# An adaptive-layer-norm block with log-sparse attention: other filler matmuls in the setup, the FFN weight's quantisation on ScalarE and GpSimd, and another order of ScalarE's and GpSimd's work in steps 0 to 2

## The chip, the cores and the metric

One core of a Trainium2 chip runs the kernel. The metric is the device time of one execution in microseconds (us), the median of three runs. A profiled execution gives the trace; its clock starts at the first instruction.

## The reference

Eight batches of 512 tokens by 256 channels (L = 512, D = 256), 16 heads of 16 channels, all in f32:

```python
mod = (silu(c) @ wmod).reshape(8, 6, 1, -1)      # sa, ca, ga, sb, cb, gb
ga, gb = sign * maximum(abs(.), 0.25)            # both gates
h = layernorm(x) * (1 + ca) + sa
q, k, v = h @ Wq.T + bq, h @ Wk.T + bk, h @ Wv.T + bv
scores = where(log_sparse_mask, q @ k.T, 0) / sqrt(16)   # j = i or j = i - 2**k
x = x + ga * (softmax(scores) @ v @ Wo.T + bo)
h = layernorm(x) * (1 + cb) + sb
x = x + gb * (dequant(fp6(h)) @ dequant(fp6(W)).T + bias)
```

`fp6` takes blocks of 32 values, scales each by its largest magnitude over 7.5 and rounds to the nearest of the 64 values of the format. A token attends with a score of its own to ten positions (itself and 1, 2, 4, ... 256 back); every other position counts with a score of zero.

## The kernel before, in words

**Setup.** The first batch is normalised, the weights are transposed by TensorE, and VectorE quantises the FFN weight (`setup_ffn_weight`: block maxima, scale, inverse, product, fp8 code, product back). Then VectorE makes the products of q and k of batch 0 (`first_qk_products`, L1710) and the rows of the modulation. TensorE fills waits with matmuls that nothing reads (`keep_busy`, three rows by 512 columns of bf16). GpSimd makes constants, the reciprocal root of batch 0 and later that of batch 1.

**Steps.** Then a loop of steps b = 0 to 5 runs on every engine, and an unrolled tail. Each engine's queue is written out by hand and runs in order; engines meet by semaphores alone. In step b:

- VectorE takes the maximum of the scores of batch b (L1802), subtracts it (L1806), waits for ScalarE's exponentials, makes the weights (L1819 to L1827), and then alternates the ten products of weights and v of batch b (`pv_product`, L1851) with the ten products of q and k of batch b + 1 (L1721).
- GpSimd adds the nine products of batch b to the first (`add`, L677), scales the projection's weight by the gate of batch b (`gate_projection`, L626), takes the reciprocal roots for batch b + 3 before attention and batch b - 1 after it (`rstd_before`, `rstd_both`), and from step 2 on modulates (L375, L380).
- ScalarE evacuates v, k, h and the attention from PSUM, takes sums and squares for both layer norms (L1188, L1197, L1217, L1238), normalises (`norm_before`, `norm_after`, L1174), takes the exponentials (`exps`), copies the scores of batch b + 1 (`copy_scores`, L1444, L1446) and puts q's bias into PSUM (`seed_q`).
- TensorE makes q and v of batch b + 1, transposes h of b + 2 and the attention of b - 1, projects, makes k of b + 2, sums the products over channels (`head_sums`, L937, L951) and transposes the scores (L963, L966).
- SyncE issues every transfer, in order: x of batch b + 3 (L414, after batch b + 2 is normalised), the spill of v and its seven shifted copies (L458, L466), each shifted copy after the product that frees its buffer, and between them rows such as the next gate row (L438), which waits for the gate product of batch b.

So in step b = 1 SyncE's order is: x of batch 4, spill of v, shifted copies 1 and 2, columns, copy 3, bias, residual x, copy 4, gate row of batch 2, copies 5, 6 and 7. Step 0 has the gate row of batch 1 in the same place, ahead of its copies 5 to 7.

Of the kernel before, what the change touches and what calls it, by code (L numbers as in the profile page):

```python
# [26 lines left out]
def adaln_block(nc, x, wq, bq, wk, bk, wv, bv, wo, bo, wf, bf, cond, wmod, out):  # L27
# [41 lines left out]
    with ExitStack() as ctx:  # L69
# [3 lines left out]
        def sem(name):  # L73
            return ctx.enter_context(nc.semaphore(name))
# [127 lines left out]
        s_xtile = sem("first_x_norm_tiles_by_scalar")  # L202
        s_xtiled = sem("first_x_norm_tiles_by_vector")
        s_split = sem("gated_biases_split")
        s_xin = sem("x_in_loaded")
# [84 lines left out]
        CONST_ALL = CONST_SUM + NO + 2  # L290
        SETUP_SILU, SETUP_COLS, SETUP_WF, SETUP_MOD, SETUP_ROWS = 3, 5, 11, 12, 16
        PE_COND, PE_MOD, PE_WK, PE_COLS, PE_WQ, PE_WV, PE_ROWS, PE_WO, PE_WF = range(1, 10)
# [276 lines left out]
        def _(pool):  # L569
# [25 lines left out]
            for n in range(1, NO):  # L595
# [5 lines left out]
                                    ALU.add).then_inc(s_const, 1)  # L601

            def split_gated_biases():

                pool.wait_ge(s_cset, SETUP_ROWS)
                nc.gpsimd.tensor_copy(split8[:, 0], gated8[:, :, :]).then_inc(s_split, 1)
                pool.wait_ge(s_split, 1)
                nc.gpsimd.tensor_tensor(rest8[:, :, :], gated8[:, :, :], split8[:, 0], ALU.subtract).then_inc(s_split, 1)
                pool.wait_ge(s_split, 2)
                nc.gpsimd.tensor_copy(split8[:, 1], rest8[:, :, :]).then_inc(s_split, 1)  # L610
                pool.wait_ge(s_split, 3)
                nc.gpsimd.tensor_tensor(rest8[:, :, :], rest8[:, :, :], split8[:, 1], ALU.subtract).then_inc(s_split, 1)
                pool.wait_ge(s_split, 4)
                nc.gpsimd.tensor_copy(split8[:, 2], rest8[:, :, :]).then_inc(s_split, 1)
# [79 lines left out]

            rstd_before(0)
            rstd_before(1)
            split_gated_biases()
            for b in range(LAST - 1):
                if has(b - 2):
                    modulate(pool, nc.gpsimd, b - 2)  # L700
                if has(b - 3):
                    gate_ffn(b - 3)
                if b == 0:
                    rstd_before(2)
                add(b, 1)
                add(b, 2)
                add(b, 3)
                add(b, 4)
                gate_projection(b)
                add(b, 5)  # L710
                add(b, 6)
                if has(b + 3) and has(b - 1):
                    rstd_both(b)
                elif has(b + 3):
                    rstd_before(b + 3)
                elif has(b - 1):
                    rstd_after(b - 1)
                add(b, 7)
                add(b, 8)
                add(b, 9)  # L720
            modulate(pool, nc.gpsimd, LAST - 3)
            gate_ffn(LAST - 4)
# [20 lines left out]
        @block.tensor  # L743
        def _(pe):
            pe.wait_ge(s_const, CONST_EARLY)
            for j in range(NC):
# [7 lines left out]

            keep_busy(ps67, 1, 3)
            pe.wait_ge(s_cond, 16)
            for k in range(NC):
                mm = nc.tensor.transpose(ps23[:, 0, B * k:B * k + B], cond_sb[:, P * k:P * k + P], ident[0:B, 0:B])
            mm.then_inc(s_pset, 1)
            keep_busy(ps67, 1, 4)  # L760

# [8 lines left out]
            def weight_transposes(i):  # L770

                pe.wait_ge(s_w_in[i], 16)
                if i == 2:
                    pe.wait_ge(s_cset, SETUP_COLS)
                if i == 3:
                    pe.wait_ge(s_d, 1)
                if i == 4:
                    pe.wait_ge(s_cset, SETUP_WF)
                    pe.wait_ge(s_x1, 1)
                for k in range(NC):  # L780
                    for c in range(NC):
                        mm = nc.tensor.transpose(turned_weight(i)[:, k, P * c:P * c + P], w_raw[:, i, c, P * k:P * k + P],
                                                 ident[:, :])
                mm.then_inc(s_pset, 1)
# [378 lines left out]
        def _(act):  # L1163
# [3 lines left out]
            def evacuate_weight(i):  # L1167
                act.wait_ge(s_pset, {2: PE_WV, 3: PE_WO, 4: PE_WF}[i])
                nc.scalar.activation(wT[:, i, :, :], turned_weight(i), ACT.Copy).then_inc(s_wTe, 1)

            def norm(src, dst, rstd, shift, done, tiles=slice(0, NT)):

# [280 lines left out]
            evacuate_weight(2)  # L1453
            evacuate_k(0, 0)
            sums_before(1)
            squares_before(1)
# [6 lines left out]
            seed_q(1)  # L1463
            centre_h(1)

            for b in range(LAST - 1):
                ahead, norm1 = has(b + 2), has(b + 3)
                exps(b)
                if has(b - 1):
                    mean_of_v(b - 1)  # L1470
# [5 lines left out]
                if has(b - 2) and has(b + 2):  # L1476
                    norm_after(b - 2)
                evacuate_v(b + 1, 1)
                if b == 0:
                    norm_before(2)  # L1480
# [12 lines left out]
                if has(b - 1):  # L1493
                    take_x1(b - 1)
                if ahead:
                    evacuate_k(b + 2, 1)
# [12 lines left out]
                if b == 1:  # L1509
                    evacuate_weight(4)  # L1510
                if has(b - 1):
                    squares_after(b - 1)
# [5 lines left out]
                if has(b + 2):  # L1518
                    seed_q(b + 2)
                if has(b + 3):  # L1520
                    norm_before(b + 3)
                elif has(b - 1):
                    norm_after(b - 1)
# [56 lines left out]
        def _(dve):  # L1580
# [87 lines left out]
            def setup_rows():  # L1668

                link, k = chain(s_cset, 0, 0)  # L1670
                k[0] = SETUP_WF
                dve.wait_ge(s_pset, PE_ROWS)
# [14 lines left out]

            def setup_ffn_weight():
                link, k = chain(s_cset, 0, 0)
                k[0] = SETUP_COLS  # L1690

                dve.wait_ge(s_w_in[4], 16)
                dve.wait_ge(s_const, 3)
                wf_b = w_raw[:, 4, :, :].rearrange("p c (g k) -> p (c g) k", k=BLOCK)
                wf_qb = wf_q[:, :].rearrange("p (g k) -> p g k", k=BLOCK)
                link(nc.vector.tensor_reduce(wf_amax[:, :], wf_b, AX_X, ALU.max, apply_absolute_value=True))
                link(nc.vector.tensor_scalar(wf_scale[:, :], wf_amax[:, :], TO_E4M3 / FP6_MAX, TO_E4M3 * MX_EPS,
                                             ALU.mult, ALU.max))
                link(nc.vector.reciprocal(wf_inv[:, :], wf_scale[:, :]))
                link(nc.vector.tensor_tensor(wf_b, wf_b, over(wf_inv[:, :], BLOCK), ALU.mult))  # L1700
                link(nc.vector.tensor_scalar(wf_q[:, :], w_raw[:, 4, :, :].rearrange("p c k -> p (c k)"), TIE_DOWN,
                                             None, ALU.add, saturate=False))
                link(nc.vector.tensor_tensor(wf_b, wf_qb, over(wf_scale[:, :], BLOCK), ALU.mult))
                assert k[0] == SETUP_WF

# [148 lines left out]

            setup_ffn_weight()
            first_qk_products(1)
# [106 lines left out]
```

## Time and profile before

| | |
|---|---|
| median of 3 runs | 286.82 us (286.75 to 286.82) |
| profiled execution, its own time | 286.72 us |
| its span | 285.0 us |
| busy: TensorE | 255.6 us (90%) |
| busy: VectorE | 258.8 us (91%) |
| busy: ScalarE | 212.5 us (75%) |
| busy: GpSimd | 210.5 us (74%) |
| maxima of scores (start of steps 0, 1, 2, 3 on VectorE) | 32.11, 59.49, 88.53, 117.86 us |

PE is TensorE's matmul queue, PEld its weight loads, DVE VectorE, ACT ScalarE, POOL GpSimd and SPq SyncE's queue of transfers. A busy share is a mean over the whole span; the timelines below are what shows who waits where.

### The profile page before, as it was taken

The page shows a single profiled execution, that of the slowest core. Times are in us where ns is not written, and L with a number is a line of the kernel's source. Part 1 is how long each engine was busy: PE and PEld are TensorE (multiplying, and loading weights), DVE is VectorE, ACT ScalarE, POOL GpSimd, SP SyncE. Part 2 cuts the span into 40 slices and gives each one's busy share as a digit, 9 for nine tenths or more (in the row PEclk, how much of TensorE's full clock was granted, in tenths as well). Part 3 has the DMA queues.
Part 4 walks back from the last instruction along what each step waited for, and adds up shares of the span by engine and source line. Part 5 has one row for each costly group of instructions (what it writes and reads, how often), then busy time and mean ns, then how long its engine had stood idle before and what let it go on. Part 6 is the DMA issues. An engine that isn't in the chain of part 4 may idle for free.

```text
span 285.0 us, 4442 instructions
## 1 busy us (share of the span) xinstructions
PE 255.6 (90%) x1368; PEld 158.8 (56%) x1368; DVE 258.8 (91%) x326; ACT 212.5 (75%) x577; POOL 210.5 (74%) x152
## 2 busy tenths in 40 slices
PE   6999997697978795989999999999999988997885
PEld 1653554175526561666556646664567646794663
DVE  3699799969995999999999999999999999999970
ACT  2386987975697779879898989887776937575752
POOL 7101439895879999999999999999999699845100
PEclk9999999999999999999999999999999999999999
DMA  7743977694784239724993389347943965730005
GB/s 225 193 181 81 340 248 232 230 338 133 240 273 148 73 125 350 251 72 131 295 336 127 129 263 286 135 113 222 333 147 94 279 198 178 230 103 11 0 26 199
DMA packets 54399, 53.91 MB, mean 189 GB/s; under 512 B 4100, under 2 KB 52824, under 8 KB 54376
## 3 DMA queue, kind: packets, MB, share of 16 engines
q1 hardware_dynamic: 54376, 53.63, 60.1%
q8 instruction: 11, 0.18, 0.3%
q14 instruction: 12, 0.10, 0.1%
HBM read 44.90 MB, written 8.72 MB: 188 GB/s over the span
## 4 chain that ended last, share of the span: by engine, by line
DVE 39%; POOL 19%; PE 18%; issue 11%; ACT 11%; DVEq 0%; POOLq 0%; ACTq 0%
POOL pv_buf L677 14%; DVE prod L1721 9%; DVE pv_buf L1851 9%; DVE prod L1851 4%; DVE prod L1710 4%; PE ps L988 3%; PE ps L1067 3%; PE ps L826 2%; ACT dump L1197 2%; PE ps L853 2%; ACT dump L1238 1%; DVE ps L1825 1%; PE ps L837 1%; DVE ps L1827 1%; POOL rstd L658 1%
## 5 line engine op out<-in xcount | busy, mean ns | idle before, releaser
L677 POOL TENSOR_TENSOR pv_buf<-pv_buf 128x1024 f32<-128x1024 f32 (+2 forms) x60 | 132.5, 2209 | 15.0 <-DVE pv_buf L1851 9.8
L1721 DVE TENSOR_TENSOR prod<-ps,kT 128x1024 f32<-128x1024 f32 (+4 forms) x70 | 75.1, 1110 | 0.0
L1851 DVE TENSOR_TENSOR pv_buf<-v_shift,ps 128x1024 f32<-128x1024 f32 x49 | 59.1, 1212 | 0.0
L937 PE MATMUL ps<-prod,sel_sum 128*32 128x512 f32 x256 | 30.8, 598 | 8.5 <-DVE prod L1721 7.8
L853 PE MATMUL ps<-wT,h_cen 128*128 128x256 f32 x128 | 29.9, 379 | 0.0
L826 PE MATMUL ps<-hT,wT 128*128 128x512 f32 x64 | 29.7, 596 | 0.0
L837 PE MATMUL ps<-hT,wT 128*128 128x512 f32 x64 | 29.3, 599 | 0.0
L988 PE MATMUL ps<-wo_g,w_raw 128*128 128x256 f32 x112 | 27.9, 392 | 0.0
L853 PEld LDWEIGHTS ps<-wT,h_cen 128*128 128x128 f32 x128 | 23.9, 190 | 6.4 <-issue 3.8
L988 PEld LDWEIGHTS ps<-wo_g,w_raw 128*128 128x128 f32 x112 | 20.1, 189 | 5.4 <-issue 3.2
L937 PEld LDWEIGHTS ps<-prod,sel_sum 128*32 128x32 f32 x256 | 6.7, 109 | 28.0 <-issue 13.8
L1067 PE MATMUL ps<-wf_g,w_raw 128*128 128x256 f32 x80 | 19.7, 391 | 0.0
L1851 DVE TENSOR_TENSOR pv_buf<-v_base,ps 128x1024 f32<-128x1024 f32 (+2 forms) x21 | 19.4, 950 | 0.2
L1291 ACT ACTIVATE kT<-ps,bias_cols 128x512 f32<-128x512 f32 x16 | 10.9, 686 | 11.6 <-PE ps L826 11.6
L649 POOL TENSOR_TENSOR rstd<-var,minus_half 128x4 f32<-128x4 f32 x4 | 4.1, 1016 | 20.1 <-ACT var L1201 19.3
L1174 ACT ACTIVATE x_norm<-x_in,shift,rstd 128x256 f32<-128x256 f32 x28 | 14.5, 594 | 5.6 <-POOL shift L651 3.2
L837 PEld LDWEIGHTS ps<-hT,wT 128*128 128x128 f32 x64 | 11.7, 190 | 12.4 <-issue 12.4
L826 PEld LDWEIGHTS ps<-hT,wT 128*128 128x128 f32 x64 | 11.6, 190 | 10.5 <-issue 9.0
L1067 PEld LDWEIGHTS ps<-wf_g,w_raw 128*128 128x128 f32 x80 | 14.5, 189 | 3.6 <-issue 2.0
L1174 ACT ACTIVATE x_norm<-x,shift,rstd 128x256 f32<-128x256 f32 x28 | 14.5, 592 | 1.4 <-POOL shift L668 1.4
L380 POOL TENSOR_TENSOR h<-x_norm,rows_mod 128x1024 f32<-128x1024 f32 x6 | 14.2, 2362 | 0.5
L375 POOL TENSOR_TENSOR x_norm<-x_norm,rows_mod 128x1024 f32<-128x1024 f32 x6 | 14.2, 2364 | 0.3 <-ACT x_norm L1174 0.2
(212 smaller groups left out, 550.3 us busy)
## 6 DMA issues: line engine op xcount, KB each, us to landing
v_shift<-v_rows SPq DMA_DIRECT2D x56, 512.0 KB, 5.7
x_in<-in_L_attn_x SPq DMA_DIRECT2D x8, 512.0 KB, 4.4
v_rows<-v_base SPq DMA_DIRECT2D x8, 512.0 KB, 4.1
x_res<-in_L_attn_x SPq DMA_DIRECT2D x8, 512.0 KB, 6.5
out_x<-outb SPq DMA_DIRECT2D x5, 512.0 KB, 5.8
rows_mod<-mod_rows SPq DMA_DIRECT2D x7, 256.0 KB, 3.4
x<-in_L_wmod SPq DMA_DIRECT2D x1, 1024.0 KB, 7.9
row_ga<-mod_rows SPq DMA_DIRECT2D x8, 128.0 KB, 4.9
```

The source lines that it names most:

```text
L375: ops.tensor_tensor(normed[:, t, :], normed[:, t, :], rows[:, 0:1, :].broadcast_to([P, n, D]), ALU.mult).then_inc(scaled, 1)
L380: ops.tensor_tensor(dst[:, t, :], normed[:, t, :], rows[:, 1:2, :].broadcast_to([P, n, D]), ALU.add).then_inc(done, 1)
L677: nc.gpsimd.tensor_tensor(dst, dst, ring(b, n)[:, t:NT, :], ALU.add).then_inc(s_add, 1)
L826: mm = nc.tensor.matmul(ps23[:, j, :], wT[:, 1, k, P * j:P * j + P], hT[:, k, :], start=(k == 1), stop=(k == 0))
L837: mm = nc.tensor.matmul(ps01[:, j, :], wT[:, 0, k, P * j:P * j + P], hT[:, k, :], start=False, stop=(k == NC - 1), skip_group_check=True)
L853: mm = nc.tensor.matmul(ps23[:, k2, col:col + D], h_cen[:, k, P * t:P * t + P], wT[:, 2, k, :], start=(t % 2 == 0 and k == 0), stop=(t % 2 ...
L937: mm = nc.tensor.matmul(ps23[32 * g:32 * g + 32, 1, :], sel_sum[:, which, c, :], prod[:, n, c, :], start=(c == 0 and which == 0), stop=(c ...
L988: mm = nc.tensor.matmul(ps[:, k2, col:col + D], attnT[:, k, P * t:P * t + P], wo_by[b][:, k, :], start=False, stop=(t % 2 == 1 and k == NC ...
L1067: mm = nc.tensor.matmul(ps[:, half_, col:col + D], xdT_by[b][:, k, P * t:P * t + P], wf_by[b][:, k, :], start=False, stop=(t % 2 == 1 and ...
L1174: ins = nc.scalar.activation(dst[:, t, :], src[:, t, :], ACT.Identity, scale=rstd[:, t:t + 1], bias=shift[:, t:t + 1])
L1721: nc.vector.tensor_tensor(prod[:, n, :, o:L], ps01[:, :, o:L], kT[:, b % 2, :, 0:L - o], ALU.mult).then_inc(s_prod, 1)
L1851: nc.vector.tensor_tensor(dst[:, t:NT, :].rearrange("p t (h e) -> p t h e", e=DH), v_n.rearrange("p t (h e) -> p t h e", e=DH), weights, A ...
```

## The change

TensorE's filler: three matmuls of the 128 by 128 identity with itself as soon as it is made, ahead of the matmuls that open q's banks; one where three thin fillers stood; three where four stood. VectorE keeps three operations of the FFN weight's quantisation; GpSimd takes the two products and ScalarE the fp8 code, joined by a new semaphore, and the weight's transposes in step 1 wait for it. On ScalarE the centring of h of batch 1 moves behind the exponentials of step 0. The normalising of batches 3 and 4 moves from the end of steps 0 and 1 into steps 1 and 2, behind the exponentials and the first evacuation of v. The squares of x1 of steps 1 and 2 move to right behind the taking of x1, ahead of k's evacuation, so the scores' copies follow other work. On GpSimd the gate product of steps 0 and 1 moves behind the last addition, and in step 0 the reciprocal root for batch 3 too, ahead of the gate.

```diff
@@ gpsimd
+            def scale_ffn_weight(src, factor, after):
+                pool.wait_ge(s_wfq, after)
+                nc.gpsimd.tensor_tensor(w_raw[:, 4, :, :].rearrange("p c (g k) -> p (c g) k", k=BLOCK),
+                                        src.rearrange("p (g k) -> p g k", k=BLOCK), over(factor[:, :], BLOCK),
+                                        ALU.mult).then_inc(s_wfq, 1)
...
             rstd_before(0)
+            scale_ffn_weight(w_raw[:, 4, :, :].rearrange("p c k -> p (c k)"), wf_inv, WF_SCALED - 1)
+            scale_ffn_weight(wf_q[:, :], wf_scale, WF_CODES)
             rstd_before(1)
...
                 add(b, 4)
-                gate_projection(b)
+                if b > 1:
+                    gate_projection(b)
                 add(b, 5)
                 add(b, 6)
                 if has(b + 3) and has(b - 1):
                     rstd_both(b)
-                elif has(b + 3):
-                    rstd_before(b + 3)
                 elif has(b - 1):
                     rstd_after(b - 1)
...
                 add(b, 9)
+                if b == 0:
+                    rstd_before(3)
+                if b < 2:
+                    gate_projection(b)
@@ tensor
+            def warm_up(ps, bank, n):
+                for i in range(n):
+                    nc.tensor.matmul(ps[:, bank, 0:P], ident[:, :], ident[:, :], start=True, stop=True)
+
+            pe.wait_ge(s_const, 2)
+            warm_up(ps67, 1, 3)
             pe.wait_ge(s_const, CONST_EARLY)
...
-            keep_busy(ps67, 1, 3)
+            warm_up(ps67, 1, 1)
             pe.wait_ge(s_cond, 16)
...
-            keep_busy(ps67, 1, 4)
+            warm_up(ps67, 1, 3)
...
                 if i == 4:
-                    pe.wait_ge(s_cset, SETUP_WF)
+                    pe.wait_ge(s_wfq, WF_DONE)
                     pe.wait_ge(s_x1, 1)
@@ scalar
+            def ffn_weight_codes():
+                act.wait_ge(s_wfq, WF_SCALED)
+                act.wait_ge(s_const, 3)
+                nc.scalar.activation(wf_q[:, :], w_raw[:, 4, :, :].rearrange("p c k -> p (c k)"), ACT.Identity,
+                                     bias=tie[:, 0:1], saturate=False).then_inc(s_wfq, 1)
...
             evacuate_k(0, 0)
+            ffn_weight_codes()
             sums_before(1)
...
-            centre_h(1)
...
                 exps(b)
+                if b == 0:
+                    centre_h(1)
...
                 evacuate_v(b + 1, 1)
+                if 0 < b < TAIL - 1:
+                    norm_before(b + 2)
...
                     take_x1(b - 1)
+                    if b < TAIL - 1:
+                        squares_after(b - 1)
...
-                if has(b - 1):
+                if has(b - 1) and b >= TAIL - 1:
                     squares_after(b - 1)
...
-                if has(b + 3):
+                if b >= TAIL - 2 and has(b + 3):
                     norm_before(b + 3)
-                elif has(b - 1):
+                elif b >= TAIL - 2 and has(b - 1):
                     norm_after(b - 1)
@@ vector
-                link(nc.vector.tensor_tensor(wf_b, wf_b, over(wf_inv[:, :], BLOCK), ALU.mult))
-                link(nc.vector.tensor_scalar(wf_q[:, :], w_raw[:, 4, :, :].rearrange("p c k -> p (c k)"), TIE_DOWN,
-                                             None, ALU.add, saturate=False))
-                link(nc.vector.tensor_tensor(wf_b, wf_qb, over(wf_scale[:, :], BLOCK), ALU.mult))
```

TAIL is 4. The three operations that stay on VectorE (maxima, scale, inverse) keep their place and form.

## Rows read from the trace of the kernel before

**Rows 1.** Chain of waits: start us, us, what.
```profile
14.63 0.70 DVE w_raw L1700
...
16.55 2.23 DVE prod L1710 x4
...
85.15 0.91 POOL pv_buf L677
...
123.60 1.06 PE ps L893 x8
```

**Rows 2.** Timeline, TensorE: start us, us, engine, line, op, out<-in, xcount.
```profile
3.19 1.48 PE L752 MATMUL ps<-ones 3*128 3x512 bf16 x3
...
9.37 1.97 PE L800 MATMUL ps<-ident,x_norm 128*128 128x128 f32 x8
...
11.12 1.06 PE L782 MATMUL ps<-ident,w_raw 128*128 128x128 f32 x4
...
12.17 1.95 PE L826 MATMUL ps<-hT,wT 128*128 128x512 f32 x4
...
13.96 1.88 PE L837 MATMUL ps<-hT,wT 128*128 128x512 f32 x4
...
29.50 1.09 PE L813 MATMUL ps<-ident,x_norm 128*128 128x128 f32 x8
```

**Rows 3.** Timeline, GpSimd, steps 0 to 2; in brackets the idle time before, and its releaser.
```profile
51.99 1.27 POOL L626 TENSOR_TENSOR wo_g<-wT,row_ga 128x512 f32<-128x512 f32 x1
...
69.25 7.39 POOL L677 TENSOR_TENSOR pv_buf<-pv_buf 128x1024 f32<-128x1024 f32 x3 [3.07 <-DVE pv_buf L1851]
...
85.15 2.36 POOL L677 TENSOR_TENSOR pv_buf<-pv_buf 128x1024 f32<-128x1024 f32 x1 [2.06 <-DVE pv_buf L1851]
```

**Rows 4.** One line's instructions: duration ns min/median/max, first and last start us.
```profile
L1421 ACT ACTIVATE q_last<-v_shift,tie x2: 722/722/722, 270.7 to 274.4; 128x512 fp8e4<-128x512 f32 x2
```

**Rows 5.** Timeline, VectorE and ScalarE, seams of step 0.
```profile
35.21 0.50 DVE L1819 TENSOR_TENSOR ps<-ps,em 128x320 f32<-128x320 f32 x1 [1.29 <-ACT ps L1433]
...
56.25 0.60 ACT L1444 ACTIVATE score_buf<-ps 128x512 f32<-128x512 f32 x1 [0.25 <-PE ps L937]
...
59.49 0.89 DVE L1802 TENSOR_REDUCE mx<-ps 128x64 f32<-128x704 f32 x1
```

**Rows 6.** Timeline, VectorE, waits for exponentials in steps 1 and 2.
```profile
63.49 0.50 DVE L1819 TENSOR_TENSOR ps<-ps,em 128x320 f32<-128x320 f32 x1 [2.19 <-ACT ps L1433]
...
92.41 0.50 DVE L1819 TENSOR_TENSOR ps<-ps,em 128x320 f32<-128x320 f32 x1 [2.06 <-ACT ps L1433]
```

**Rows 7.** Windows, GpSimd: stretch, its length, busy us (x instructions), clock, DMA.
```profile
88.00:117.00 29.00, 27.98 (x15) 1.00 0.59 192
```

**Rows 8.** Timeline, SyncE's queue, end of step 0 and step 1.
```profile
54.94 0.50 SPq L438 DMA_DIRECT2D row_ga<-mod_rows  x1
...
62.62 0.37 SPq L414 DMA_DIRECT2D x_in<-in_L_attn_x  x1
```

**Rows 9.** Timeline, ScalarE, step 1.
```profile
72.26 0.41 ACT L1188 ACTIVATE dump<-x_in 128x256 f32<-128x256 f32 x1
...
75.04 0.39 ACT L1217 ACTIVATE x<-ps 128x256 f32<-128x256 f32 x1 [0.36 <-PE ps L988]
...
76.75 0.69 ACT L1291 ACTIVATE kT<-ps,bias_cols 128x512 f32<-128x512 f32 x1 [0.87 <-PE ps L826]
...
78.47 0.69 ACT L1291 ACTIVATE kT<-ps,bias_cols 128x512 f32<-128x512 f32 x1 [1.03 <-PE ps L826]
...
82.97 0.58 ACT L1169 ACTIVATE wT<-ps 128x512 f32<-128x512 f32 x1
...
85.89 0.58 ACT L1444 ACTIVATE score_buf<-ps 128x512 f32<-128x512 f32 x1
```

**Rows 10.** Transfers into x_in, then into v_shift: us from issue to landing.
```profile
DMA to landing us min/median/max: 3.2/3.8/6.1
...
DMA to landing us min/median/max: 2.1/5.6/9.2
```

More of the change, by code:

```diff
@@ L203, in adaln_block @@
         s_xtiled = sem("first_x_norm_tiles_by_vector")
+        s_wfq = sem("ffn_weight_quantising_step")
         s_split = sem("gated_biases_split")
@@ L290, in adaln_block @@
         CONST_ALL = CONST_SUM + NO + 2
-        SETUP_SILU, SETUP_COLS, SETUP_WF, SETUP_MOD, SETUP_ROWS = 3, 5, 11, 12, 16
+        SETUP_SILU, SETUP_COLS, SETUP_MOD, SETUP_ROWS = 3, 5, 6, 10
+        WF_SCALED, WF_CODES, WF_DONE = 4, 5, 6
         PE_COND, PE_MOD, PE_WK, PE_COLS, PE_WQ, PE_WV, PE_ROWS, PE_WO, PE_WF = range(1, 10)
@@ L1670, in setup_rows @@
                 link, k = chain(s_cset, 0, 0)
-                k[0] = SETUP_WF
+                k[0] = SETUP_COLS
                 dve.wait_ge(s_pset, PE_ROWS)
@@ L1686, in setup_rows, with ffn_weight_scales @@
                 assert k[0] == SETUP_ROWS
-            def setup_ffn_weight():
-                link, k = chain(s_cset, 0, 0)
-                k[0] = SETUP_COLS
+            def ffn_weight_scales():
                 dve.wait_ge(s_w_in[4], 16)
-                dve.wait_ge(s_const, 3)
                 wf_b = w_raw[:, 4, :, :].rearrange("p c (g k) -> p (c g) k", k=BLOCK)
[L1695 to L1699, printed above, removed]
-                link(nc.vector.tensor_tensor(wf_b, wf_b, over(wf_inv[:, :], BLOCK), ALU.mult))
-                link(nc.vector.tensor_scalar(wf_q[:, :], w_raw[:, 4, :, :].rearrange("p c k -> p (c k)"), TIE_DOWN,
-                                             None, ALU.add, saturate=False))
-                link(nc.vector.tensor_tensor(wf_b, wf_qb, over(wf_scale[:, :], BLOCK), ALU.mult))
-                assert k[0] == SETUP_WF
+                nc.vector.tensor_reduce(wf_amax[:, :], wf_b, AX_X, ALU.max,
+                                        apply_absolute_value=True).then_inc(s_wfq, 1)
+                dve.wait_ge(s_wfq, 1)
+                nc.vector.tensor_scalar(wf_scale[:, :], wf_amax[:, :], TO_E4M3 / FP6_MAX, TO_E4M3 * MX_EPS,
+                                        ALU.mult, ALU.max).then_inc(s_wfq, 1)
+                dve.wait_ge(s_wfq, 2)
+                nc.vector.reciprocal(wf_inv[:, :], wf_scale[:, :]).then_inc(s_wfq, 1)
             def first_qk_products(c):
@@ L1853, in pv_product @@
                                         ALU.mult).then_inc(s_pv, 1)
-            setup_ffn_weight()
+            ffn_weight_scales()
             first_qk_products(1)
```

## The prediction

> **What bounds the kernel now.** I read four views in this order. The chain of waits comes first, since it says which engine sets the end in which stretch. In the setup it runs over VectorE: the FFN weight is scaled and quantised there, right ahead of the first products of q and k [rows 1]. Through steps 1 and 2 (up to about 123 us) it runs over GpSimd's additions, then it enters TensorE's transposes of the attention at 123.60 and stays on TensorE and ScalarE for the next two steps [rows 1]. So what the change gives early counts only as far as it moves the first q and k products and, later, GpSimd's last addition of step 2. Second, the timeline of TensorE in the setup shows its rate [rows 2]. Third, the timelines of GpSimd, VectorE and ScalarE show who waits at the seams of steps 0 to 2 [rows 3 to 6, 9]. Last, the SyncE queue and the landing times show what the moved gate holds back [rows 8, 10].
>
> All times below are on the clock of the profiled execution: span 285.0 us, its own time 286.72, so 1.7 us lie outside the span. The median of the runs is 286.82, 0.10 more. I subtract the gain from the median.
>
> **Setup: the FFN weight leaves VectorE.** Three of its six operations go (scale, code, scale back), 14.63 to 16.55: 1.92 us [rows 1]. They become a GpSimd product, a ScalarE activation and a second GpSimd product. GpSimd is idle then; a product of this shape takes 1.27 us there [rows 3], so the first runs from about 14.6 to 15.9. ScalarE's code operation, 0.72 us for this shape [rows 4], stands behind the second k evacuation and delays the statistics of batch 1; ScalarE waits for scores later in the setup, which hides it. The weight's transposes come only in step 1, so this route costs nothing as long as these idle stretches are there, and at most 0.7 us without them. The gain is not 1.92: VectorE would be free at 14.63, but the first product needs q. TensorE's four passes for it start at 13.96 and end at 15.84 [rows 2], after which 16.55 becomes 15.85. The floor of this term is 0.7 us.
>
> **Setup: deep instead of thin filler.** Seven fillers of 3 rows by 512 columns go, and seven of 128 by 128 come, two groups of them at other places. TensorE's rate is low until about 12.2: eight transposes take 1.97 us at 9.37, and eight of the same shape take 1.09 at 29.50 [rows 2]. The recorded granted clock says 1.00 for the whole span and does not show this, but spacings of 0.21 us against 0.11 are the two levels, 1.2 and 2.4 GHz. The thin fillers (three in 1.48 us) were running then [rows 2], and did not raise it; the rise came behind the full-height transposes at 9.37 and 11.12 [rows 2]. The fill is the one unknown of the setup. If the rise stays at 12.2, the term is 0.7. If it comes before 9.37, the eight transposes lose 0.9, the weight's four at 11.12 come at 10.4 and lose 0.5, q ends at 14.7 and the term is 1.8, with VectorE still in time (its three remaining weight operations end near 13.6). The new fillers are shorter in total, so they delay nothing; I bound a loss at 0.2 (one filler of 0.2 us in front of a real matmul). I take a rise inside the transposes, about 10.3: four of them and the weight's four run fast, q ends at about 15.3, term 1.2.
>
> The Trainium skill, page "TensorE: Matmul & The Clock Gate", section "Part 4: PE-mode transpose", says transposes don't engage the full clock, not counting as busy in the same way. The rows disagree: the work from 9.37 to 12.17 was transposes only, and the group at 12.17, four passes in 1.95 us, ran at the rate of every later one (0.43 us a pass) [rows 2]. By the page alone only the new real matmuls would count, which speaks for the early rise, 1.8.
>
> **Step 0: exponentials before centring.** VectorE waits 1.29 us for the exponentials, which stand behind the centring of h [rows 5]. They now start with the maximum, and VectorE goes on at about 34.0 instead of 35.21: some 1.25 earlier. But centring, k, and the statistics of batch 2 then end 0.4 later on ScalarE, and ScalarE is next: its first copy of scores stood at 56.25 after only 0.25 of waiting [rows 5]. With VectorE's products early and ScalarE 0.4 late, the second copy ends at about 57.5 instead of 57.7, and the maximum of step 1 starts at 59.3 rather than 59.49. Of 1.25 us 0.2 stay.
>
> **Step 1.** GpSimd no longer has the gate (1.27 us) and the root among its additions of step 0. It waited there for products anyway: the sixth addition can start with its product, 1.25 earlier than now, at 55.6, and ends at 58.0 by 2.36 us each [rows 3]; three more of 1024, 768 and 512 columns take 5.7. The last ends near 63.7 instead of 66.2 (69.25 less the wait of 3.07 [rows 3]), then the root ends at 65.0 and the gate at 66.25, inside that wait. ScalarE's exponentials no longer wait behind the normalising of batch 3: the 2.19 us at 63.49 [rows 6] go, and 0.2 from step 0 comes to it: VectorE runs 2.4 ahead in step 1. The normalising itself falls into ScalarE's wait for the attention's transposes.
>
> Now the queue. SyncE's load of the next gate row stood at 54.94 [rows 8]; it waits for the gate product, so it comes at 66.3, and with it three shifted copies of v (0.5 MB each) and the load of x for batch 4, which is 62.62 in the profile [rows 8] and becomes about 68.2. Landings of x take 3.2 to 6.1 us [rows 10]; behind four other transfers I take the upper end, 74.3. ScalarE would be ready for it at 71.5 (72.26 now [rows 9]), so a new wait of some 2.8 us arises. From there to the variance it has work of 85.89 - 72.26 = 13.6, less the three waits of 0.36, 0.87 and 1.03 and the weight's copy of 0.58, which now comes behind: 10.8 [rows 9]. It ends at 85.1. GpSimd's sixth addition, started at 85.15 now behind a wait of 2.06 for the product [rows 3], starts 2.4 earlier and ends at 85.1 too. So the new wait just fits, with nothing to spare, and the root starts at 85.1, 2.4 earlier than 87.5.
>
> **Step 2.** The wait of 2.06 for the exponentials goes as well [rows 6], but GpSimd is the engine that decides: from 85.15 it works without a pause into step 3, as its 27.98 busy microseconds of 29 show [rows 7] (the missing one is spread over the hand-overs), and the chain lies on it [rows 1]. The gate of step 1, which lay before a wait, now lies in the unbroken part: +1.27. 2.4 - 1.27 = 1.1 us earlier at the last addition, and so at the transposes of 123.60 [rows 1]. The gate row of step 2 and x for batch 5 are again late (x lands near 102, ScalarE waits 2), but its variance is due 1.8 before GpSimd asks. From step 3 on the order is the old one and the difference stays.
>
> **Sum.** 1.2 (setup) + 1.1 (steps 0 to 2) = 2.3; 286.82 - 2.3 = 284.5.
>
> **Rivals.**
> (a) The clock rises where it did: for it, the new fillers last 1.5 us in all against 3 for the thin ones, with gaps. 0.7 + 1.1: 285.0.
> (b) It rises before 9.37: 1.8 + 1.1: 283.9. For it, full-height work is what preceded the rise.
> (c) x of batch 4 arrives too late: slower. The place is ScalarE's sum at 72.26. From 74.3 on each microsecond goes on to GpSimd's root; the gain is used up at 76.6. Shifted copies of v took up to 9.2 us to land [rows 10]; with that, x lands at 77.4, 3.1 late: -2.3 + 3.1 = +0.8, 287.6, and a second late x in step 2 (9.2 us from 95.9, its margin of 1.8 and a landing of 102 leave 1.3 over) makes it up to 288.9. Against it: no load of x took over 6.1.
> (d) The changes of steps 0 to 2 give VectorE nothing, because ScalarE is late from other work, while the gate of step 1 costs GpSimd its 1.27: +1.27 - 1.2: 286.9, no change. Against it: the two waits of 2.19 and 2.06 have one cause, and it is removed.
>
> **How the numbers follow.** Chances: forecast 0.42, (a) 0.21, (b) 0.15, (c) 0.14, (d) 0.08. What a measurement of this kernel tells from no change is about 0.2%, 0.57 us. Faster holds the first three, slower (c), same (d) and none else: 0.78, 0.08, 0.14. The likeliest alone ranges from 283.9 to 285.3 (each term 0.6). The range for 8 in 10 goes from 283.4, (b) with another 0.5 from waits I put down as hidden, to 286.9, which takes in (d) and leaves (c) out.
>
> **What would show it right or wrong.** VectorE's first product of q and k at about 15.3 (15.85 in (a), 14.7 in (b)), and eight h transposes in under 1.6 us. No wait of VectorE for exponentials in steps 0 to 2 over 0.3 us. The load of x for batch 4 at about 67 on SyncE (everything in the steps is 1.2 earlier by the setup), a ScalarE wait of 2 to 3 us before its sums, and GpSimd's transposes-releasing addition of step 2 at 121.1 rather than 123.4. It is wrong if GpSimd waits for the variance in step 1, if the steps from 3 on do not keep a constant distance, or if the clock falls in the setup once it has risen.

## The result and the profile after

| | before | after |
|---|---|---|
| median of four runs each | 286.78 us (286.54 to 286.82) | 290.66 us (290.18 to 291.31) |
| profiled execution, its own time | 286.72 us | 290.18 us |
| its span, mean granted clock of TensorE | 285.0 us, 1.00 | 288.5 us, 0.97 |
| maxima of scores start at | 32.11, 59.49, 88.53, 117.86 us | 30.43, 59.70, 89.45, 122.07 us |

The ratio is 1.0138 (1.0117 to 1.0160): slower, where 284.5 us was forecast. Here and below a ratio leaves out an execution over 1.5% above the fastest of its kernel (one with the gate rows moved, one with ScalarE's old order), while a median keeps it. The four maxima say in which step the time goes. The setup gives 1.7 us. Steps 0 and 1 take that back and 0.9 more, step 2 costs another 3.3, and from step 3 on the distance is 3.5 us in every step (151.77 against 148.28, 243.05 against 239.57).

Timeline of VectorE, kernel after; it answers to [rows 1, 5, 6]:

```profile
14.88 10.98 DVE L1734 TENSOR_TENSOR prod<-ps,kT 128x512 f32<-128x512 f32 x20 [1.71 <-PE ps L856]
...
59.70 0.89 DVE L1826 TENSOR_REDUCE mx<-ps 128x64 f32<-128x704 f32 x1 [3.07 <-PE ps L985]
...
61.72 0.50 DVE L1843 TENSOR_TENSOR ps<-ps,em 128x320 f32<-128x320 f32 x1 [0.21 <-ACT ps L1458]
...
89.45 0.89 DVE L1826 TENSOR_REDUCE mx<-ps 128x64 f32<-128x704 f32 x1 [3.56 <-PE ps L985]
...
122.07 0.89 DVE L1826 TENSOR_REDUCE mx<-ps 128x64 f32<-128x704 f32 x1 [5.06 <-PE ps L985]
```

The first product starts 1.67 us earlier, and the wait for exponentials is 0.21 instead of 2.19 [rows 6]. But VectorE now stands 3 to 5 us ahead of each of the next three maxima, for scores that TensorE has not made. Timeline of TensorE, kernel after; the first four rows answer to [rows 2]:

```profile
1.58 1.65 PE L760 MATMUL ps<-ident 128*128 128x128 f32 x6 [1.58 <-POOL minus_half L578]
...
9.13 1.09 PE L819 MATMUL ps<-ident,x_norm 128*128 128x128 f32 x8
...
12.96 1.88 PE L856 MATMUL ps<-hT,wT 128*128 128x512 f32 x4
...
43.07 1.97 PE L832 MATMUL ps<-ident,x_norm 128*128 128x128 f32 x8 [2.49 <-ACT x_norm L1199]
...
57.88 1.78 PE L985 MATMUL ps<-fold,score_buf 128*128 128x48 f32 x8
...
112.59 6.28 PE L956 MATMUL ps<-prod,sel_sum 128*32 128x512 f32 x32 [5.04 <-DVE prod L1745]
```

Three things are to be seen. The first eight transposes take 1.09 us: in this execution the clock has risen before 9.13. The same eight transposes take 1.97 at 43.07, behind a wait of 2.49: it has fallen again. And at 112.59 TensorE, which went on with these sums at 107.29 in the kernel before, has waited 5.04 us and makes all 32 matmuls at once, in 6.28 us; before, they were two groups of 1.92.

Windows, TensorE, kernel after: stretch, its length, busy us (x instructions), granted clock, DMA share, GB/s:

```profile
43.10:46.50 3.40, 3.40 (x14) 0.53 0.79 191
56.80:63.60 6.80, 6.63 (x17) 0.52 0.40 129
107.70:111.40 3.70, 0.00 (x0) 0.96 0.43 127
111.40:118.20 6.80, 5.61 (x28) 0.52 1.10 349
```

In three stretches the granted clock is at the low one of its two levels (1.2 of 2.4 GHz), two of them right behind a wait of TensorE. The Trainium skill, page "TensorE: Matmul & The Clock Gate", section "HAM oscillation — how this bites in real kernels", describes this: work that is cut up by waits for data starts again at the low rate after each. The row at 112.59 agrees. The row at 43.07 agrees only in part: its wait of 2.49 us is shorter than those of the page's example, and a kernel further down has the same wait at the same place and keeps its clock.

Why TensorE waits at 107.7 is seen upstream. Timeline of SyncE's queue, kernel after; it answers to [rows 8]:

```profile
65.19 0.35 SPq L440 DMA_DIRECT2D row_ga<-mod_rows  x1
...
69.46 0.37 SPq L416 DMA_DIRECT2D x_in<-in_L_attn_x  x1
...
95.26 0.33 SPq L440 DMA_DIRECT2D row_ga<-mod_rows  x1
95.64 1.54 SPq L468 DMA_DIRECT2D v_shift<-v_rows  x3
97.32 0.59 SPq L416 DMA_DIRECT2D x_in<-in_L_attn_x  x1
```

Timeline of ScalarE, kernel after, x of batches 4 and 5, and k's evacuation of batch 4; it answers to [rows 9]:

```profile
75.53 0.42 ACT L1213 ACTIVATE dump<-x_in 128x256 f32<-128x256 f32 x1 [1.91 <-DMA x_in<-in_L_attn_x]
...
106.17 0.42 ACT L1213 ACTIVATE dump<-x_in 128x256 f32<-128x256 f32 x1 [4.70 <-DMA x_in<-in_L_attn_x]
...
111.82 1.25 ACT L1316 ACTIVATE kT<-ps,bias_cols 128x512 f32<-128x512 f32 x2
```

Transfers into x_in, kernel after (3.2/3.8/6.1 in [rows 10]):

```profile
DMA to landing us min/median/max: 3.3/4.8/8.8
```

The gate row now stands at 95.26, three shifted copies of 0.5 MB leave within 1.54 us behind it, and x right behind them. It is there only 8.8 us after its issue, and ScalarE waits 4.70 us. Behind that wait ScalarE takes x1 and, in the new order, its squares, and only then evacuates k: at 111.82, where it was 105.68. `head_sums` of the next batch waits for the first half of k's evacuation (`s_k`), which ends at 112.44: by the kernel's waits, that frees TensorE at 112.59. The profile writes this wait to VectorE's product, which came at about the same time; but the first 16 of these matmuls need no such late product (they ran at 107.29 before). Timelines of TensorE and ScalarE, kernel before:

```profile
107.29 1.92 PE L937 MATMUL ps<-prod,sel_sum 128*32 128x512 f32 x16
...
111.45 1.92 PE L937 MATMUL ps<-prod,sel_sum 128*32 128x512 f32 x16 [2.24 <-DVE prod L1721]
...
105.68 0.69 ACT L1291 ACTIVATE kT<-ps,bias_cols 128x512 f32<-128x512 f32 x1 [0.88 <-PE ps L826]
```

Timeline of GpSimd, kernel after; it answers to [rows 3]:

```profile
86.40 1.65 POOL L666 TENSOR_TENSOR rstd<-var,minus_half 128x8 f32<-128x8 f32 x1 [0.62 <-ACT var L1226]
...
93.97 1.27 POOL L634 TENSOR_TENSOR wo_g<-wT,row_ga 128x512 f32<-128x512 f32 x1
...
117.04 1.65 POOL L666 TENSOR_TENSOR rstd<-var,minus_half 128x8 f32<-128x8 f32 x1 [1.14 <-ACT var L1226]
...
118.93 5.74 POOL L685 TENSOR_TENSOR pv_buf<-pv_buf 128x1024 f32<-128x1024 f32 x3
```

GpSimd's last addition of step 2 ends at 118.93 + 5.74 = 124.67; 121.1 was forecast, and 123.45 is the kernel before. It waits for the variance in step 1 (0.62 us) and in step 2 (1.14 us), where the prediction had it wait in neither. But this is not the path that sets the end: the maximum of step 3 is 4.2 us late and GpSimd's addition 1.2, and in the chain that ended last GpSimd has 1% of the span, where it had 19% before.

### The profile page after: what moved, and what is told of

Read it like the earlier page. It is cut to its first block, busy times and chain, and to the rows that moved or that the text cites. A ratio compares the mean times of both kernels' runs of the same rounds, so it can differ in the third digit from the quotient of the medians.

```text
span 288.5 us, 4456 instructions
## 1 busy us (share of the span) xinstructions
PE 261.4 (91%) x1375; PEld 164.7 (57%) x1375; DVE 256.8 (89%) x323; ACT 213.1 (74%) x578; POOL 212.5 (74%) x154
## 4 chain that ended last, share of the span: by engine, by line
DVE 48%; PE 24%; ACT 14%; issue 10%; DMA 2%; POOL 1%; DVEq 0%; ACTq 0%; POOLq 0%
DVE prod L1745 12%; DVE pv_buf L1875 12%; DVE prod L1734 4%; PE ps L856 4%; DVE prod L1875 4%; PE ps L845 3%; ACT dump L1222 3%; PE ps L1086 3%; PE ps L956 2%; DMA x_in<-in_L_attn_x 2%; DVE mx L1826 2%; PE ps L872 2%; ACT dump L1213 2%; DVE ps L1849 2%; DVE ps L1851 1%
## 5 line engine op out<-in xcount | busy, mean ns | idle before, releaser
L956 PE MATMUL ps<-prod,sel_sum 128*32 128x512 f32 x256 | 33.0, 643 | 7.9 <-DVE prod L1745 7.7
L856 PE MATMUL ps<-hT,wT 128*128 128x512 f32 x64 | 31.3, 632 | 0.0
L845 PE MATMUL ps<-hT,wT 128*128 128x512 f32 x64 | 29.9, 599 | 0.5 <-ACT hT L1290 0.5
L956 PEld LDWEIGHTS ps<-prod,sel_sum 128*32 128x32 f32 x256 | 7.8, 116 | 28.5 <-issue 16.6
L856 PEld LDWEIGHTS ps<-hT,wT 128*128 128x128 f32 x64 | 12.5, 204 | 13.6 <-issue 13.6
L845 PEld LDWEIGHTS ps<-hT,wT 128*128 128x128 f32 x64 | 11.9, 195 | 10.7 <-issue 10.0
L1826 DVE TENSOR_REDUCE mx<-ps 128x64 f32<-128x704 f32 x8 | 7.1, 888 | 11.8 <-PE ps L985 11.7
L1323 ACT ACTIVATE v_base<-ps 128x512 f32<-128x512 f32 x16 | 9.4, 593 | 9.6 <-PE ps L872 9.6
L1213 ACT ACTIVATE dump<-x_in 128x256 f32<-128x256 f32 x28 | 11.2, 406 | 6.6 <-DMA x_in<-in_L_attn_x 6.6
```

Of the source, the lines that this page charges most:

```text
L845: mm = nc.tensor.matmul(ps23[:, j, :], wT[:, 1, k, P * j:P * j + P], hT[:, k, :], start=(k == 1), stop=(k == 0))
L856: mm = nc.tensor.matmul(ps01[:, j, :], wT[:, 0, k, P * j:P * j + P], hT[:, k, :], start=False, stop=(k == NC - 1), skip_group_check=True)
L956: mm = nc.tensor.matmul(ps23[32 * g:32 * g + 32, 1, :], sel_sum[:, which, c, :], prod[:, n, c, :], start=(c == 0 and which == 0), stop=(c ...
L1213: ins = nc.scalar.activation(dump[:, t, :], x_in[:, t, :], ACT.Identity, accum_out=sum1[:, t:t + 1])
```

## The experiments

Two theories were tested. The first: the moved gate product holds the gate row back in SyncE's in-order queue, the shifted copies crowd x, and x's lateness passes over ScalarE to TensorE. The second: the new filler and the new order of ScalarE drop TensorE's clock, and that is the loss. All ratios (of means) are to the kernel before, on the same chip, with the 95% interval; differences in us are of medians. The kernel before had medians of 286.62 to 286.82 us on these chips.

**Only the queue: the gate rows of batches 1 and 2 are issued behind x.**

```diff
 load_x(b + 3)
+if 0 < b < 3: load_row_ga(b)
...
-load_row_ga(b + 1)
+if b > 1: load_row_ga(b + 1)
```

> The changed kernel with the gate rows of batches 1 and 2 issued right behind x of batches 4 and 5 on SyncE, so that neither the shifted copies of v nor x wait for the gate product. Queue theory (the loss comes from x of batches 4 and 5 arriving late): ScalarE's waits of 1.9 and 4.7 us for x go, TensorE's wait of 5.0 in step 2 goes with them, and with it the fall of the clock at 111 us: the maximum of step 3 comes near 117, the time is 284 to 286. Clock theory (the loss comes from TensorE's clock falling in steps 0 and 1, whatever the queue does): the falls near 43 and 57 us stay, together worth 3 us; the maximum of step 3 comes near 119 and the time is 287 to 288.5.

Measured: 288.29 us, 1.0045 (1.0007 to 1.0084); ScalarE's waits for x are gone, and with them TensorE's wait and the fall of its clock near 111. 2.4 of the 3.9 us come back. That is less than the first theory asked for (284 to 286); the number lies in the range of the second, but the falls near 43 and 57 us that the second foretold are not in this profile either (its first fall in the steps is at about 70 us). Timeline of TensorE, this kernel:

```profile
44.66 1.14 PE L835 MATMUL ps<-ident,x_norm 128*128 128x128 f32 x8 [2.49 <-ACT x_norm L1202]
```

The wait is the 2.49 us of the kernel after, and the eight transposes behind it run at the high clock. From the maximum of step 0 to that of step 1 it takes 58.89 - 32.03 = 26.9 us, against 29.3 in the kernel after. On the other hand its setup was slow in this execution: the first product started at 16.47.

**Only GpSimd: the gate product back behind the fourth addition.**

```diff
 add(b, 4)
-if b > 1: gate_projection(b)
+gate_projection(b)
...
-if b < 2: gate_projection(b)
```

> The changed kernel with the gate product of steps 0 and 1 back behind the fourth addition (the root for batch 3 stays behind the last). Queue theory: as with the gate rows moved, the waits for x go, 284 to 286.5. Clock theory: 287 to 289, falls near 43 and 57 us stay.

Measured: 286.49 us, 0.9966 (0.9937 to 0.9996): 4.2 us less than after. The falls near 43 and 57 us stay, as the second theory had it, but the time is in the range of the first. Timelines of SyncE and ScalarE, this kernel:

```profile
54.92 0.53 SPq L440 DMA_DIRECT2D row_ga<-mod_rows  x1
...
70.17 0.37 SPq L416 DMA_DIRECT2D x_in<-in_L_attn_x  x1
...
74.22 0.42 ACT L1210 ACTIVATE dump<-x_in 128x256 f32<-128x256 f32 x1
```

x is issued no earlier than in the kernel after (69.46), since it waits for the normalising that moved behind the exponentials. But it lands within 4.05 us, without a wait, as its copies have long gone out. So in the kernel after it is the crowd of transfers ahead of x that makes this load late, and not its issue. For batch 5 the issue is hardly earlier either (96.48 against 97.32), and x is read at 100.52 without a wait.

**The old fillers in the kernel after, the new ones in the kernel before.** (`keep_busy(ps67, 1, 3)` and `(…, 4)` for the three `warm_up`, and the reverse.)

> The changed kernel with the thin fillers of before in the setup. Its setup is 0.9 us later by the late rise of the clock (first product of q and k at 15.8 instead of 14.9). Queue theory: the waits for x stay, and the time is 291.5. Clock theory: the falls in steps 0 and 1 hang on when TensorE's waits fall relative to the rise in the setup; with the late rise they go or move, and the time is 288 to 290.

> The kernel before with the deep fillers alone. Queue theory: the clock rises near 9 us, VectorE's quantising then ends near 15.6 instead of 16.55 and the time is 285.8 to 286.1, no fall later. Clock theory: the rise moves by over 3 us, the waits of steps 0 to 2 now stand differently to it, and a fall of some microseconds at the low level appears in step 0 or 1: 287 to 289.

Measured: 291.02 us, 1.0132 (1.0083 to 1.0182) with thin fillers, and 286.78 us, 1.0000 (0.9972 to 1.0029) for the kernel before with deep ones, though its first product starts at 15.82 instead of 16.55. The filler of the setup neither made the loss nor gives a gain. (286.78 lies below the second theory's 287 to 289 and above the first's 285.8 to 286.1; most executions of this kernel have a clock of 0.97 to 0.993.) Waits by name, thin fillers: us, count, largest:

```profile
ACT dump L1211 <- DMA x_in<-in_L_attn_x: 8.4, 2, 5.5
```

The waits for x are there as before (8.4 us in all, against 6.6 in the kernel after). That speaks for the first theory.

**More filler in step 0's waits, with and without the late gate.**

```diff
+if b == 0: pe.wait_ge(s_d, 1); warm_up(ps67, 1, 8)
 h_transposes(b + 2, 1)
...
 v_means(b)
+if b == 0: warm_up(ps67, 0, 5)
```

> The changed kernel with the gate product back behind the fourth addition and, in step 0, eight deep fillers ahead of TensorE's transposes of h of batch 2 and five ahead of its transposes of the scores of batch 1, where it waited 2.5 and 1.8 us. Theory (queue first, clock second): the queue's share is gone by the gate, and the fillers keep the clock up near 43 and 57 us, so the maximum of step 1 comes at 58.5 instead of 60.15 and the time is 284.3 to 285.2. Rival (the clock's falls cost nothing, since other waits hide them): 286.2 to 286.8, as without fillers.

> The changed kernel with those same fillers and nothing else. Queue first: no fall near 43 and 57 us, but the waits of ScalarE for x of batches 4 and 5 stay and grow by what steps 0 and 1 gain, so 290 to 291. Clock first: 288 to 289, most of the loss gone.

Measured: with the gate product back, 286.82 us, 0.9988 (0.9922 to 1.0054); with it late, 289.59 us, 1.0084 (1.0023 to 1.0145). The kernel with the gate back missed its 284.3 to 285.2: by the median, the fillers in step 0 gained nothing over the 286.49 without them, which is the rival's range. The one with the late gate lies between its two theories. In the profile of the first of them the clock does not fall in steps 0 to 2 (the kernel with the gate rows moved shows that it may also stay up there without filler). Timelines of VectorE and TensorE, that kernel:

```profile
113.75 0.88 DVE L1828 TENSOR_REDUCE mx<-ps 128x64 f32<-128x704 f32 x1
...
121.25 1.91 PE L909 MATMUL ps<-ident,pv_buf 128*128 128x128 f32 x8 [2.71 <-POOL pv_buf L685]
```

VectorE enters step 3 4.1 us ahead of the kernel before, but TensorE then waits 2.71 us for GpSimd's additions, its clock falls there, and the next maximum is at 147.60, only 0.7 ahead of 148.28. So GpSimd's chain decides the entry into step 3, as the prediction had it, and time won above it is lost in that wait.

**The kernel before with the late gate product and nothing else; then also with the gate rows behind x** (the two diffs above, on the kernel before).

> The kernel before with one edit: the gate product of steps 0 and 1 behind the last addition. Queue theory: the gate row of step 0 is issued at 67 to 68, x of batch 4 at about 69 instead of 62.6, ScalarE waits 2 to 3 us for it, in step 1 the same again with 3 to 5 us: 289 to 291. Rival (it takes ScalarE's new order to make x late): no wait for x over 1 us, 286.8 to 288 (the gate product itself is 1.3 us more on GpSimd in step 2).

> The kernel before with the gate product of steps 0 and 1 behind the last addition, as in the run that lost 6 us, and now the two gate rows issued behind x of batches 4 and 5 on SyncE. Queue theory (the loss comes from transfers held back behind the gate row): x lands in time as before, the loss shrinks from 6 to 1.3 us or less (what the gate product adds to GpSimd in step 2): 286.8 to 288.3. Rival (the loss comes from the gate product's place on GpSimd): 291 or more.

Measured: 292.88 us, 1.0198 (1.0144 to 1.0251), and 289.06 us, 1.0078 (1.0036 to 1.0119). The late gate alone is above even the queue theory's 289 to 291; with the rows behind x the time lies between the two theories. The one move of the gate costs more alone than the whole change does. SyncE's queue with the late gate alone, and its waits:

```profile
67.36 0.35 SPq L438 DMA_DIRECT2D row_ga<-mod_rows  x1
...
69.33 1.14 SPq L414 DMA_DIRECT2D x_in<-in_L_attn_x  x1
```

```profile
ACT dump L1191 <- DMA x_in<-in_L_attn_x: 8.5, 2, 5.9
```

The same queue with the rows reordered as well:

```profile
62.88 0.37 SPq L414 DMA_DIRECT2D x_in<-in_L_attn_x  x1
...
67.67 0.34 SPq L438 DMA_DIRECT2D row_ga<-mod_rows  x1
```

With the product as late as before but x at its old place (62.62 in [rows 8]) there is no wait for x, and 3.9 of 6.3 us are back (each against the kernel before on the same chip). Of the 2.4 left, 1.4 are GpSimd's own, as the start of its root of step 2 shows, for the gate's 1.27 now lies in its unbroken part. Timelines of GpSimd, the kernel before and then this one:

```profile
115.80 1.66 POOL L658 TENSOR_TENSOR rstd<-var,minus_half 128x8 f32<-128x8 f32 x1
```

```profile
117.22 1.65 POOL L661 TENSOR_TENSOR rstd<-var,minus_half 128x8 f32<-128x8 f32 x1
```

The rest, about 1 us, I can't name; the granted clock was 0.986 in that profile.

**The kernel after with ScalarE's old order; and the setup of the change alone.**

```diff
-if b == 0: centre_h(1)        # goes back ahead of the loop
-if 0 < b < TAIL - 1: norm_before(b + 2)
...
-if b < TAIL - 1: squares_after(b - 1)
+squares_after(b - 1)      # at its old place, behind k
+norm_before(b + 3)        # at the end of the step
```

> The changed kernel with ScalarE's order of before in the steps (setup, root and gate as changed). Queue theory: x is late as in the changed kernel, 287.5 to 290.5. Rival (ScalarE's new order is what loses): 285 to 286.5, the setup's gain alone.

> The change's setup alone (deep fillers, FFN weight on ScalarE and GpSimd), with the steps as before. If a gain of the setup is carried to the end: first product of q and k at 14.9 to 16.2, 285.1 to 286.1. If the clock's falls take it back: a fall of 3.4 us or more in some executions, 286.2 to 287.5.

Measured: 295.75 us, 1.0266 (1.0192 to 1.0340), and 286.79 us, 0.9984 (0.9943 to 1.0024). The first is outside both its ranges: ScalarE's new order is worth 5 us next to the late gate (4 by the ratios), so it is good, not the loss. The setup alone is worth nothing that can be measured.

**The change without anything of GpSimd's new order in the steps** (gate and root back at their old places).

> The changed kernel with GpSimd's whole order of before (gate and root at their old places), ScalarE's new order and the new setup. Theory (ScalarE's order gains where nothing is late): as with the gate alone moved back, 286.0 to 286.8, waits for exponentials gone, GpSimd's sixth addition of step 1 ends near 85. Rival (the root behind the last addition is needed for ScalarE's new order): 287 or more.

Measured: 285.84 us (284.09 to 286.99), 0.9946 (0.9908 to 0.9985): faster than before, and 4.8 us less than after. From the kernel with only the gate back (286.49, 0.9966) it can't be told apart by these intervals. Its executions scatter, and the scatter goes with the granted clock. Windows, TensorE, the profiled execution of this kernel (286.81 us, clock 0.97):

```profile
43.00:46.40 3.40, 3.03 (x13) 0.51 0.83 197
56.70:63.50 6.80, 6.28 (x17) 0.50 1.10 347
```

Single executions, by their granted clock:

```
kernel                 clock 1.00                 0.976              0.970
before (79 runs)       286.66 (28 runs)           287.81 (9)         289.37 (7)
gate and root back     284.09 (1)                 285.59-285.99 (5)  286.56-286.99 (4)
```

The kernel before has 31 more executions at 0.986 to 0.994; their median is 286.62 us, as at 1.00. So in that kernel falls of this size cost nothing by the medians, and only the larger ones go with longer times.

**Filler where the records show falls, on the last kernel, and on the kernel before.** (The fillers of step 0 as above, on the kernel before with the setup's deep ones too, nine ahead of step 3's attention transposes, five in the tail in place of thin ones.)

> The changed kernel with GpSimd's order of before in steps 0 and 1, and deep fillers in TensorE's waits: eight and five in step 0, nine ahead of the transposes of the attention in step 3, five in the tail in place of three thin ones. Clock theory: granted clock 0.985 or more in most executions instead of 0.970 to 0.976, median 284.1 to 285.0. Rival (fillers delay TensorE by as much): median 285.8 or more.

> The kernel before with the deep fillers of the setup and the same fillers in steps 0 and 3 and the tail. Clock theory: its executions of 288 to 290 go, median 286.0 to 286.5 (the setup's 0.7 comes through). Rival: TensorE has no room there (its waits are shorter, 2.1 us and less in step 0), and the median rises over 287.

Measured: 285.19 us (283.17 to 286.49), 0.9907 (0.9868 to 0.9946), the best version, near the clock theory's range and ahead of both kernels; five of its twelve runs had a clock of 1.00 and took 283.17 to 283.78. On the kernel before, the same fillers cost time, as its rival had it: 288.01 us, 1.0039 (1.0008 to 1.0070). Timeline of TensorE, the best version:

```profile
42.12 1.95 PE L757 MATMUL ps<-ident 128*128 128x128 f32 x16
...
44.78 1.14 PE L829 MATMUL ps<-ident,x_norm 128*128 128x128 f32 x8 [0.71 <-ACT x_norm L1204]
...
121.59 1.06 PE L909 MATMUL ps<-ident,pv_buf 128*128 128x128 f32 x8
```

The transposes behind the filler take 1.14 and 1.06 us, where they took 1.97 at 43.07 (kernel after) and 1.91 at 121.25 (filler in step 0 alone). That filler is what keeps the clock up rests on the clocks of all executions and not on these rows: 0.982 or more in all twelve here, 0.976 or less in nine of ten without it. The times follow less clearly: the executions here at 0.987 took 285.41 to 286.32 us, no less than those at 0.976 without filler. Filler pays where a wait is there to fill. In the kernel before, the wait of 2.07 us ahead of the transposes of h takes the eight fillers; but its transposes of the scores stood at 57.88 without a wait, and there the five fillers (1.36 us) stand in front of work. In the same profile the clock also fell just before them (sums that take 1.04 us took 1.96 at 55.80). The maximum of step 1 comes at 61.46, behind a wait of 2.81, instead of 59.49; filler and fall both have a share in it.

## Why the prediction was wrong, step by step

**The setup** went further than the forecast in the profiled execution (1.67 us against 1.2), since the clock rose before 9.13, which was rival (b). That was luck of this execution: in the profiles of the eight other kernels with the same setup and the same work in it, the first product starts between 15.17 and 16.59 (16.55 before), and the eight transposes take 1.09 to 1.97 us. One step behind the forecast was mis-sized: I put the seven fillers at 1.5 us in all. A matmul of two 128 by 128 f32 matrices leaves two records (x6 for three), and three take 1.65 us at the low clock; with the single one's 0.80, the seven make 1.65 + 0.80 + 1.65 = 4.1. So TensorE was kept busier than I thought, and the new fillers are longer in total than the thin ones (1.48 + 1.86 = 3.3 us), not shorter. What the setup gives does not reach the end by itself: the kernels with deep filler alone and with the setup alone equal the kernel before. The term of 1.2 us in the sum failed there: 0 is what it is worth at the end by those two runs.

**Step 0** was forecast to keep 0.2 us; it gave back 1.9 (59.70 - 30.43 = 29.3 us between the maxima, 27.4 before). The prediction looked for falls of the clock in the setup alone. In the step TensorE waits 2.49 us for the normalising of h, and the clock falls at 43.1 and again at 56.8. Where it does not fall behind the same wait, as in the profile of the kernel with the gate rows moved, the step takes 26.9 us, 0.5 less than before, so the falls are what the step's forecast left out. Why the clock falls in one execution and not in the other stays open.

**The waits for exponentials** are gone as forecast. ScalarE's order is what the kernel with GpSimd's old order (285.84 us) has over the setup alone (286.79), though the intervals of the two ratios overlap.

**The queue** was the right place with the wrong margin. For batch 4 the forecast was a load issued at about 67, landed at 73, and a wait of 2 to 3 us: it was 69.46, 75.53 and 1.91. The issue was 2.5 us late because this load also waits for ScalarE's normalising of batch 3, which the change had moved behind the exponentials; the prediction counted the gate row and the copies alone. Where the prediction failed is its sentence that in step 2 the variance "is due 1.8 before GpSimd asks". It had x land near 102, 6.1 us behind its issue, where 106.17 and 8.8 came; the variance was 1.14 us too late for GpSimd instead of 1.8 early. And it followed x only as far as the variance. It did not ask what else is queued behind x on ScalarE: the squares of x1 had just been moved ahead of k's evacuation, so k waits for x too, TensorE for k (5.04 us), and its clock falls on that wait (6.28 us for 3.84 of matmuls). That x comes too late is rival (c), but over another path: it let GpSimd's root wait, and GpSimd's last addition of step 2 is only 1.2 us later than before, while TensorE's sums make the next maximum 4.2 later. Its price for the late x, 3.1 to 4.4 us, was about right (2.4 came back in the kernel after, 3.9 in the kernel before). Its 287.6 to 288.9 is below 290.66 since it kept the whole gain of 2.3 us, of which the run with the gate rows moved (288.29) shows nothing.

**GpSimd's gate in its unbroken part** was forecast at +1.27 us; the pair of kernels before shows +1.42 at the root of step 2.

**The sum.** Gate and root back give 4.8 us. The falls of the clock go with about 1.8 more (285.84 against the one execution at 1.00, 284.09). The forecast of 284.5 holds 1.27 us for the late gate; without it, its own terms give 283.2, so even that one execution is 0.9 above it. With filler in the waits five executions at 1.00 took 283.2 to 283.8. The late gate is shown as the main cause by removing it from the kernel after, by adding it alone to the kernel before, and by moving only the rows it holds back. That the remaining falls cost time is suggested by the clocks of single executions and not shown by a run that takes out a fall alone: filler in step 0 by itself gained nothing by its median. That filler takes most of them out is shown by the clocks of the best version. Why an execution has them or not stays open, and so does the last fall in the steps of the best version, at 217.6.

## What to carry to other kernels

Before an instruction is moved back on one engine, list the transfers that wait for it in an in-order queue and everything that is queued behind them: the cost of a small late row is the large loads behind it, which then go out in a crowd. Follow a late load through its reader to every later instruction of that engine, and to what each of them releases, not to the one consumer that comes to mind. Where a change makes TensorE wait (2.5 and 5.0 us here), price the work behind the wait at the low clock too, or fill the wait if it is really idle. And read a gain of the setup in several profiles: here the same setup put the first product at 14.88 in the profile of one kernel and at 16.59 in that of another.

## What was not expected of the hardware

- A load of 0.5 MB that follows three others of its size within 2 us took 8.8 us to land (batch 5, kernel after). With the gate product back the same load was read 4.04 us after its issue, without a wait.
- TensorE's clock fell in a kernel in which it is busy 90% of the time, and not in the same places in each execution: the kernel before took 286.66 us at a granted clock of 1.00 and 289.37 at 0.970. A fall costs the kernel less than the stretch at the low clock: between the maxima of steps 0 and 1 the kernel after has over 6 us of it and takes 2.4 us longer than the kernel with the gate rows moved, which has none there.
- In the best version the one fall left in the steps, at 217.6, comes 1.3 us behind 16 matmuls of a single column (1.92 us from 214.39), in which the record has TensorE busy. Whether these are what let it fall was not tried.
